# Later loads for `f2` and `fk`, and two scaled copies in another order

## The chip, the cores and the metric

One Trainium2 chip, one of its cores. The metric is device time in microseconds (us), the median of several executions. A core has five engines that run their own instruction streams and meet only at semaphores: TensorE (PE, matmuls; PEld is its weight load), VectorE (DVE), ScalarE (ACT), GpSimd (POOL) and SyncE (SP), which here only waits and issues DMAs.

## The reference

Three blocks follow each other on `x` (2 batches of 128 rows by 512), each added to its input:

```python
x = x + xattn(layernorm(x), ctx)   # self attention, cross attention over 2048 context rows, MLP
x = x + rwkv7(layernorm(x))        # T=2: the two batches are the two time steps of a recurrence
x = x + ffn(layernorm(x))          # 8 heads, 5 value experts and 5 output experts, top 2

# MLP at the end of xattn
z = relu(x @ fc1_w + fc1_b);  z = z @ fc2_w + fc2_b;  x = layer_norm(x + z)

# rwkv7, per step
r, w, k, v, a, g = (mix_m(x) @ W_m for m in "rwkvag")   # mix_m(x) = x + (xprev - x) * mu_m
...                                   # state update, y
y = y * sigmoid(g) @ Wo
h = layernorm(x + y) * norm_w + norm_b
out = layernorm(silu(h @ Wf + bf)) * lnf_w + lnf_b
```

All of it is float32. Some products are computed as three products of rounded halves (high times high, high times low, low times high); `parted` is that form, `natural` the plain float32 one.

## The kernel before

The whole program is one pass with no outer loop; the order on each engine is written out by hand, and each step waits on a semaphore count (`Flag.at(name)`) of what it needs. Batches are `0` and `1`, and steps of the two are interleaved.

**Weights and context** come in as blocks of 128 by 2048 floats (1 MB). They lie in 13 places of a ring in SBUF. `fetch(name)` on SP waits until the block that lay in that place before has been used by its last product, then issues the DMA. SP is in order: a fetch that waits holds all later ones. The places that matter: `f2` is in place 5 after context block `c01`; `rg` in 2 after `c12`; `rv` in 1 after `c11`; `ro` in 8 after `v2`; `rw` in 3, `rr` in 0; `fo` in 5 after `f2`; `rf` in 6 after `rk`; `fk` in 4 after `f1`; `fg` in 3 after `rw`; `fq` in 9, whose old content is read by step `v`. Vectors (biases, norms) are broadcast to 128 partitions in `bc`; the last such load (L401, flag `s_bc2`, 768 KB, called bc2 here) holds `lnf_b`, `norm_w` and `norm_b` and follows `fk` in SP's stream, with `fq` and `fg` after it. DVE waits for `s_bc2` in `norm_h(0)` (L1192, its work is L915), PE ahead of the bias row of `rf(0)` (L847), POOL ahead of adding `lnf_b` (L2057).

**Around the MLP**, PE runs `f1(0)`, `v2(1)`, `f2(0)`, then turns batch 1 and runs `f1(1)`, `f2(1)`. `f2(0)` (L629) waits for the block `f2` and feeds `add3(0)` on DVE (L1073).

**In the recurrence**, PE runs `step(0,"v")`, `step(1,"w")`, `step(1,"r")`, `step(1,"v")`, `step(0,"g")`, `lift(0)`, `step(1,"g")`, then turns `yg(0)`, `lift(1)`, `ro(0)`, turns `yg(1)`, `ro(1)`, turns `h(0)`, the bias row and `rf(0)` (L835 to L850). A step for `g` needs its mixed rows: for batch 0 ACT writes them alone (`mix0("g", 4)`, four scaled copies of 128 by 128, and it waits for `step(0,"v")`), for batch 1 ACT writes a first term (`mix1("g", 5)`, four copies, it waits for `step(1,"r")`) and POOL adds the second (L2038 to L2040). Behind them on ACT stand `row_high("bf", ...)` (rounds the bias row), `scales0()` (eight small copies that DVE's L1479 needs), a square, `own_part()`, `tanh(0,"g")`, `bonus_rows(1)`, `tanh(1,"g")` and the copies of the turned `yg`.

The product with `Wo` is `parted`: its first eight matmuls use the high rows, which ACT has copied; its last four wait for the low rows from DVE (`low_halves`, L1103). DVE's own order there is L1484, L1497, ..., L1521, L1103 for batch 0, L1525, L1183, L1188, then L915 and L921 (the norm of `h(0)`), L1111 (low half of the bias row).

Of the kernel before, what the change touches and what calls it, by code (L numbers as in the profile page):

```python
# [80 lines left out]
def build(nc, blocks, xin, vecs, cols, out):  # L81
    with ExitStack() as ctx:
# [31 lines left out]
        v, a, g, t = nc.vector, nc.scalar, nc.gpsimd, nc.tensor  # L114
# [25 lines left out]
        def bcols(w, b):  # L140
            return w[:, :, b * 128:(b + 1) * 128]
# [4 lines left out]
        def quarters(n):  # L146
            return psum[:, n, :].rearrange("p (c n) -> p c n", c=4)
# [7 lines left out]
        def vec(name):  # L155
            i = BCAST.index(name)
            return bc[:, i if i < FIRST_BC else i - FIRST_BC, :]
# [70 lines left out]
        def flags(name, *orders):  # L228
            return [Flag(sem(f"{name}{b}"), orders[b if len(orders) > 1 else 0]) for b in range(2)]
# [74 lines left out]
        prod = flags("product", ["k1", "q1.a", "q1", "e1", "n1", "v1", "em", "pv", "q2.a", "q2", "k2", "n2", "v2",  # L304
# [20 lines left out]
        def product(name):  # L325

            return name[1] if name in ("rk", "ra", "rw", "rr", "rv", "rg") else name

        def used(name):

            if name.startswith("ct"):
                return score[int(name[2])].at(name[3])
            if name[0] == "c":
                return gath[int(name[1])].at(name[2])
            return prod[1].at(product(name))
# [5 lines left out]
        @block_.sync  # L341
        def _(eng):
            s = Waits(eng)

            def fetch(name, first=False):
                before = [m for m in BLOCKS if PLACE[m] == PLACE[name] and NTH[m] == NTH[name] - 1]
                for m in before:
                    s.wait_ge(*used(m))
                    if m[0] != "c" and m != "rw":
                        s.wait_ge(*prod[0].at(product(m)))  # L350
                eng.dma_start(ring[:, PLACE[name], :], blocks[BLOCKS.index(name), :, :]).then_inc(
                    s_place[PLACE[name]], 16)

            def spread(first, end):
                return vecs[first:end, :].unsqueeze(0).broadcast_to([128, end - first, 512])

            eng.dma_start(X[0][:, 0:256], xin[0, :, 0:256]).then_inc(s_x[0], 16)
            fetch("k1")
            eng.dma_start(X[1], xin[1, :, :]).then_inc(s_x[1], 16)
            fetch("q1")  # L360
            fetch("ct01")
            eng.dma_start(colv[:, :], cols).then_inc(s_cols, 16)
            fetch("v1")
            fetch("ct00")
            fetch("q2")
            fetch("ct02")
            eng.dma_start(bc[:, 0:2, :], spread(0, 2)).then_inc(s_bc0, 16)
            fetch("ct10")
            fetch("k2")
            eng.dma_start(bc[:, 2:FIRST_BC, :], spread(2, FIRST_BC)).then_inc(s_bc1, 16)  # L370
            fetch("ct03")
            fetch("ct11")
            fetch("c03")
            fetch("ct12")
            fetch("c01")
            fetch("v2")
            fetch("ct13")
            fetch("c00")
            fetch("c10")
            fetch("c02")  # L380
            fetch("f1")
            fetch("c12")
            fetch("c11")
            fetch("c13")
            s.wait_ge(*normed[0].at("x1"))
            s.wait_ge(*normed[1].at("x1"))
            eng.dma_start(bc[:, 0:2, :], spread(FIRST_BC, FIRST_BC + 2)).then_inc(s_bf, 16)
            fetch("rk")
            fetch("ra")
            fetch("f2")  # L390
            fetch("rg")
            fetch("rv")
            fetch("ro")
            fetch("rw")
            fetch("rr")
            fetch("fo")
            fetch("rf")
            fetch("fk")
            s.wait_ge(*normed[0].at("n4"))
            s.wait_ge(*normed[1].at("n4"))  # L400
            eng.dma_start(bc[:, 2:len(BCAST) - FIRST_BC, :], spread(FIRST_BC + 2, len(BCAST))).then_inc(s_bc2, 16)  # L401
            for b in range(2):
                s.wait_ge(*prod[b].at("v"))
            fetch("fq")
            fetch("fg")
            s.wait_ge(*out_v[0].at("fin"))
            eng.dma_start(out[0, :, :], X[0]).then_inc(s_y[0], 16)
            s.wait_ge(*out_v[1].at("fin.a"))
            eng.dma_start(out[1, :, 0:256], X[1][:, 0:256]).then_inc(s_y[1], 16)
            s.wait_ge(*out_v[1].at("fin"))  # L410
            eng.dma_start(out[1, :, 256:512], X[1][:, 256:512]).then_inc(s_y[1], 16)
            s.wait_ge(s_y[0], 16)
            s.wait_ge(s_y[1], 32)
# [1180 lines left out]
        def _(eng):  # L1594
            s = Waits(eng)

            def act(o, x, func, **kw):
                return a.activation(o, x, func, **kw)  # L1598
# [48 lines left out]
            def row_high(name, loaded_):  # L1647

                i, p = row_parts[name]
                s.wait_ge(*loaded_)  # L1650
                act(bc_r[p:p + 64, i, :], vec(name)[p:p + 64, :], ACT.Copy).then_inc(*rows_a.inc(name))
# [32 lines left out]
            def mix0(m, n):  # L1684

                dst = HIGH_r[0][n % 2] if m in STEPS else MIX[0][n % 2].rearrange("p (c n) -> p c n", c=4)
                k = MUS.index(m)
                s.wait_ge(*(turn if n < 2 else turned)[0].at("n4"))
                s.wait_ge(*rest_v.at("rest"))
                if n > 1:  # L1690
                    s.wait_ge(*prod[0].at(["a", "k", "v", "r", "g"][n - 2]))
                src = bcols(T8, 0) if n > 1 else quarters(0)
                for c in range(4):
                    i = act(dst[:, c, :], src[:, c, :], ACT.Copy, scale=rest[:, 4 * k + c:4 * k + c + 1])
                i.then_inc(*mixed[0].inc(m))

            def mix1(m, n):
                dst = PART[1][n % 2] if m in STEPS else MIX[1][n % 2].rearrange("p (c n) -> p c n", c=4)
                k = MUS.index(m)
                s.wait_ge(*x_sum[1].at("n4"))  # L1700
                s.wait_ge(*prod[1].at("k" if m == "v" else ["k", "a", "w", "r", "v", "g"][n - 2]))
                for c in range(4):
                    i = act(dst[:, c, :], bcols(T10, 1)[:, c, :], ACT.Copy, scale=colv[:, 4 * k + c:4 * k + c + 1])
                i.then_inc(*mixed[1].inc(m))
# [10 lines left out]
            def by_head(b, name, o_, x, factor):  # L1715
                for h in range(8):
                    cs = slice(h * 64, (h + 1) * 64)
                    i = act(o_[:, cs], x[:, cs], ACT.Copy, scale=factor[:, h:h + 1])
                i.then_inc(*by_a[b].inc(name))

            def bonus_rows(b):
                s.wait_ge(*rk_v[b].at("sb"))
                s.wait_ge(*rk_v[b].at("vc"))
                by_head(b, "pv", v_p[b], v_p[b], sbs[b])

            def scales0():
                s.wait_ge(*rk_g[0].at("rs"))
                s.wait_ge(*rk_v[0].at("km"))
                by_head(0, "sc", y_p[0], vec("lnx_w"), rs8[0])
# [138 lines left out]
            act(w1, w1, ACT.Exp, bias=wbias[:, :], scale=WC).then_inc(*sq_a[1].inc("wexp"))  # L1868
            round_step("v", 4)
            bonus_rows(0)  # L1870
            mix0("g", 4)
            mix1("g", 5)
            s.wait_ge(*x2b_g[0].at("x2b"))
            s.wait_ge(*x2b_g[1].at("x2b"))
            row_high("bf", (s_bf, 16))
            scales0()
            s.wait_ge(*rk_v[1].at("km"))
            s.wait_ge(*rk_v[1].at("vc"))
# [254 lines left out]
```

## Time and profile before

| what | value |
|---|---|
| median of 3 runs (lowest, highest) | 225.9 us (225.85, 226.06) |
| the profiled execution's own time | 225.85 us |
| its span | 224.1 us |
| PE busy | 215.2 us, 96% |
| DVE busy | 175.9 us, 79% |
| ACT busy | 112.8 us, 50% |
| POOL busy | 102.1 us, 46% |
| DMA | 43.99 MB, mean 196 GB/s |
| granted PE clock | full in all 40 slices |
| chain that ended last | PE 78%, DVE 12%, POOL 3%, ACT 2%, issue 2%, DMA 1% |

The span runs from the first to the last recorded instruction; 1.75 us of the execution lie outside it. Rows below give the start in us from the span's start. A row of the timeline merges neighbours of one kind; a number in brackets is the idle time ahead of them and what ended it. Each float32 matmul shows as two records.

### The profile page before, as it was taken

What the parts mean: (1) busy time and instruction counts of PE and PEld (TensorE: products, weight loads), DVE (VectorE), ACT (ScalarE), POOL (GpSimd) and SP (SyncE); (2) the same over time, 40 slices, a digit from 0 to 9 for tenths busy, and PEclk for the clock granted to TensorE, in tenths of its full rate; (3) what the DMA queues carried; (4) which work ended last, traced back from release to release, by engine and by line L of the source; (5) the groups of instructions that cost most, each with busy time, mean ns of one, the idle gap of its engine ahead of it and who ended that gap; (6) DMA issues with size and microseconds to landing.
All of it is one profiled execution on the core that took longest, in us unless ns stands there. A gap on an engine that the chain in (4) does not pass through costs nothing.

```text
span 224.1 us, 3249 instructions
## 1 busy us (share of the span) xinstructions
PE 215.2 (96%) x1201; PEld 169.7 (76%) x1201; DVE 175.9 (79%) x320; ACT 112.8 (50%) x217; POOL 102.1 (46%) x90
## 2 busy tenths in 40 slices
PE   8899999999999999999999999999889899999995
PEld 7898889789988888888575757564466679798863
DVE  2156883877598988799689896799999899898971
ACT  2347522383689768944435287899413111246110
POOL 5016004760568336989440109979576218160000
PEclk9999999999999999999999999999999999999999
DMA  6999999159984499927390406608100000000002
GB/s 238 431 419 415 429 437 399 50 218 427 331 342 186 140 427 388 426 72 332 101 437 32 183 0 240 275 0 317 61 0 0 0 0 3 0 1 3 0 19 75
DMA packets 6783, 43.99 MB, mean 196 GB/s; under 512 B 880, under 2 KB 1392, under 8 KB 2032
## 3 DMA queue, kind: packets, MB, share of 16 engines
q1 hardware_dynamic: 6624, 43.66, 48.9%
q8 instruction: 9, 0.15, 0.3%
q10 hardware_dynamic: 144, 0.13, 0.2%
q14 instruction: 6, 0.05, 0.1%
HBM read 43.27 MB, written 0.52 MB: 195 GB/s over the span
## 4 chain that ended last, share of the span: by engine, by line
PE 78%; DVE 12%; POOL 3%; ACT 2%; issue 2%; DMA 1%; DVEq 0%; POOLq 0%
PE psum L422 57%; PE psum L464 15%; PE psum L426 4%; ACT slots L1598 2%; PE psum L438 1%; DVE small L905 1%; DMA slots<-xin 1%; POOL small L2049 1%; POOL small L2033 1%; PE psum L598 1%; POOL small L1921 1%; DVE slots L911 1%; DVE slots L927 1%; DVE slots L915 1%; DVE small L1159 1%
## 5 line engine op out<-in xcount | busy, mean ns | idle before, releaser
L422 PE MATMUL psum<-ring_r,slots_r 128*128 128x512 f32 x360 | 88.6, 399 | 1.7 <-DVE slots_r L1103 1.3
L422 PEld LDWEIGHTS psum<-ring_r,slots_r 128*128 128x128 f32 x360 | 66.2, 188 | 20.1 <-ACT slots_r L1598 2.9
L1926 POOL TENSOR_TENSOR ring_r<-ring,ring_r 128x640 fp32r<-128x640 f32 x21 | 43.4, 2079 | 27.6 <-ACT ring_r L1598 27.6
L1598 ACT ACTIVATE slots<-psum 128x256 f32<-128x256 f32 (+4 forms) x48 | 20.3, 452 | 59.1 <-PE psum L422 22.1
L1598 ACT ACTIVATE ring_r<-ring 128x2048 fp32r<-128x2048 f32 x23 | 43.8, 1915 | 10.4 <-PE psum L422 9.2
L422 PE MATMUL psum<-ring,slots 128*128 128x512 f32 (+5 forms) x122 | 41.4, 482 | 0.3 <-ACT slots L1598 0.3
L933 DVE TENSOR_TENSOR ring_r<-ring,ring_r 128x1408 fp32r<-128x1408 f32 x21 | 35.8, 1708 | 3.0 <-ACT ring_r L1598 2.9
L464 PE MATMUL psum<-slots,ring 128*128 128x128 f32 x320 | 37.6, 277 | 0.3 <-ACT slots L1598 0.3
L464 PEld LDWEIGHTS psum<-slots,ring 128*128 128x128 f32 x320 | 36.5, 192 | 0.9 <-ACT slots L1598 0.7
L422 PEld LDWEIGHTS psum<-ring,slots 128*128 128x128 f32 (+1 forms) x122 | 20.1, 190 | 14.7 <-issue 11.0
L1921 POOL TENSOR_TENSOR small<-small,mhalf 128x1 f32<-128x1 f32 x16 | 8.8, 550 | 43.0 <-DVE small L907 41.5
L1598 ACT ACTIVATE slots_r<-psum 128x512 fp32r<-128x512 f32 (+1 forms) x20 | 9.3, 509 | 14.0 <-PE psum L438 8.6
L1936 POOL TENSOR_TENSOR slots<-slots,bc 128x512 f32<-128x512 f32 x9 | 12.6, 1405 | 8.2 <-DMA bc<-vecs 6.9
L422 PEld LDWEIGHTS psum<-slots,ring 128*128 128x128 f32 x128 | 14.6, 192 | 0.4
L422 PE MATMUL psum<-slots,ring 128*128 128x128 f32 x128 | 14.9, 276 | 0.0
L1598 ACT ACTIVATE slots<-psum,small 128x128 f32<-128x128 f32 (+1 forms) x20 | 8.8, 529 | 8.6 <-DVE small L1265 5.9
L1932 POOL TENSOR_TENSOR ring_r<-ring,ring_r 128x704 fp32r<-128x704 f32 (+1 forms) x6 | 9.8, 1647 | 6.4 <-ACT ring_r L1598 6.4
L426 PE MATMUL psum<-ident,slots 128*128 128x128 f32 x68 | 9.6, 277 | 1.0 <-DVE slots L911 0.6
L1936 POOL TENSOR_TENSOR slots<-slots 128x512 f32<-128x512 f32 x8 | 10.1, 1275 | 0.3 <-DVE small L1474 0.2
L426 PEld LDWEIGHTS psum<-ident,slots 128*128 128x128 f32 x68 | 7.6, 140 | 2.5 <-DVE slots L911 1.1
L1943 POOL TENSOR_TENSOR slots<-slots,small 128x512 f32<-128x512 f32 x4 | 5.6, 1420 | 7.1 <-DVE small L1240 7.1
L438 PE MATMUL psum<-ident,slots 128*128 128x128 f32 x44 | 7.0, 281 | 1.7 <-DVE slots L911 1.2
(179 smaller groups left out, 253.8 us busy)
## 6 DMA issues: line engine op xcount, KB each, us to landing
ring<-blocks SPq DMA_DIRECT2D x36, 1024.0 KB, 7.3
bc<-vecs SPq DMA_DIRECT2D x1, 3072.0 KB, 16.1
bc<-vecs SPq DMA_DIRECT2D x2, 512.0 KB, 15.5
bc<-vecs SPq DMA_DIRECT2D x1, 768.0 KB, 8.4
slots<-xin SPq DMA_DIRECT2D x1, 256.0 KB, 5.1
y<-slots SPq DMA_DIRECT2D x1, 256.0 KB, 2.0
y<-slots SPq DMA_DIRECT2D x2, 128.0 KB, 1.7
slots<-xin ACTq DMA_DIRECT2D x1, 128.0 KB, 2.9
```

What stands on the lines that cost most here:

```text
L422: return t.matmul(o_, l, r, start=first, stop=last)
L426: i = t.transpose(o_[:, c * 128:(c + 1) * 128], x[:, c * 128:(c + 1) * 128], ident[:, :])
L438: i = t.transpose(psum[:, bk1 if c > 1 else bk0, o_ * 128:(o_ + 1) * 128], src[:, c * 128:(c + 1) * 128], ident[:, :])
L464: i = t.matmul(psum[:, bk, e * 128:(e + 1) * 128], w[:, c, e * 128:(e + 1) * 128], srcw[:, c, b * 128:(b + 1) * 128], start=c == 0 and (e ...
L598: i = t.matmul(bank(4 * b + n), pick_r[:, n, :], pen_r[b], start=False, stop=True, skip_group_check=True)
L933: v.tensor_tensor(ring_r[:, p, 0:CUT], ring[:, p, 0:CUT], ring_r[:, high(name), 0:CUT], ALU.subtract).then_inc(*split_low.inc(name))
L1598: return a.activation(o, x, func, **kw)
L1921: g.tensor_tensor(rs[b], mv[b][:, 1:2], mhalf[:, 0:1], ALU.pow).then_inc(*rstd[b].inc(name))
L1926: g.tensor_tensor(ring_r[:, p, CUT:], ring[:, p, CUT:], ring_r[:, high(name), CUT:], ALU.subtract).then_inc(*split_lowg.inc(name))
L1932: g.tensor_tensor(ring_r[:, PLACE[name], at_], ring[:, PLACE[name], at_], ring_r[:, high(name), at_], ALU.subtract).then_inc(*split_lowg.i ...
L1936: g.tensor_tensor(o, x, y, op).then_inc(*flag.inc(name))
L1943: return g.tensor_tensor(heads(dst), x_, w_, ALU.mult)
```

## The change

On SP, the fetch of `f2` goes behind those of `rg` and `rv`, and the fetch of `fk`, with everything behind it (bc2, `fq`, `fg`), waits for both products `g`. On ACT, the scaled copies `mix0("g", 4)` go behind `mix1("g", 5)` and `row_high("bf", ...)`.

```diff
@@ SP @@
             fetch("rk")
             fetch("ra")
-            fetch("f2")
             fetch("rg")
             fetch("rv")
+            fetch("f2")
             fetch("ro")
             fetch("rw")
             fetch("rr")
             fetch("fo")
             fetch("rf")
+            for b in range(2):
+                s.wait_ge(*prod[b].at("g"))
             fetch("fk")
             s.wait_ge(*normed[0].at("n4"))
             s.wait_ge(*normed[1].at("n4"))
@@ ACT @@
             bonus_rows(0)
-            mix0("g", 4)
             mix1("g", 5)
             s.wait_ge(*x2b_g[0].at("x2b"))
             s.wait_ge(*x2b_g[1].at("x2b"))
             row_high("bf", (s_bf, 16))
+            mix0("g", 4)
             scales0()
```

## Rows read from the trace of the kernel before

**Rows 1.** The chain that ended last, in order: start, us, what.
```profile
106.25 6.21 PE psum L422 x20
...
168.58 3.42 PE psum L422 x13
```

**Rows 2.** Timeline of SP: start, us, queue, line, what, count.
```profile
98.65 0.80 SPq L351 DMA_DIRECT2D ring<-blocks  x2
...
135.18 0.80 SPq L351 DMA_DIRECT2D ring<-blocks  x2
136.08 0.38 SPq L401 DMA_DIRECT2D bc<-vecs  x1
150.96 0.80 SPq L351 DMA_DIRECT2D ring<-blocks  x2
```

**Rows 3.** DMA issues by line: duration ns, first and last start, time to landing.
```profile
L351 SPq DMA_DIRECT2D ring<-blocks x5: 328/431/432, 98.7 to 109.9; - x5
...
DMA to landing us min/median/max: 4.7/6.8/8.8
...
L351 SPq DMA_DIRECT2D ring<-blocks x2: 327/376/426, 135.2 to 135.6; - x2
...
DMA to landing us min/median/max: 4.9/6.0/7.0
...
L401 SPq DMA_DIRECT2D bc<-vecs x1: 382/382/382, 136.1 to 136.1; - x1
...
DMA to landing us min/median/max: 8.4/8.4/8.4
...
L351 SPq DMA_DIRECT2D ring<-blocks x2: 327/376/426, 151.0 to 151.3; - x2
...
DMA to landing us min/median/max: 4.9/6.2/7.4
```

**Rows 4.** Timeline where `f2(0)` begins on PE (its first weight loads).
```profile
108.63 0.41 PEld L422 LDWEIGHTS psum<-ring,slots 128*128 128x128 f32 x2
```

**Rows 5.** Timeline of ACT, 148 to 156 us.
```profile
148.76 1.32 ACT L1598 ACTIVATE slots<-slots,small 128x128 f32<-128x128 f32 x4
149.93 1.31 ACT L1598 ACTIVATE slots<-slots,colv 128x128 f32<-128x128 f32 x4
151.11 0.64 ACT L1598 ACTIVATE bc_r<-bc 64x512 fp32r<-64x512 f32 x1
...
155.97 0.56 ACT L1598 ACTIVATE psum<-psum 128x512 f32<-128x512 f32 x1
```

**Rows 6.** Timeline of PE, 150 to 164 us.
```profile
150.72 3.59 PE L422 MATMUL psum<-ring,slots 128*128 128x512 f32 x8
...
154.67 3.70 PE L422 MATMUL psum<-ring,slots 128*128 128x512 f32 x8
158.21 0.60 PE L438 MATMUL psum<-ident,slots 128*128 128x128 f32 x4
...
159.33 2.11 PE L422 MATMUL psum<-ring_r,slots_r 128*128 128x512 f32 x8
162.72 1.21 PE L422 MATMUL psum<-ring_r,slots_r 128*128 128x512 f32 x4 [1.27 <-DVE slots_r L1103]
```

**Rows 7.** Timeline of DVE, 156 to 169 us.
```profile
156.23 0.68 DVE L1484 TENSOR_TENSOR slots<-slots,psum 128x512 f32<-128x512 f32 x1
...
161.99 0.68 DVE L1103 SCALAR_TENSOR_TENSOR slots_r<-psum,slots_r 128x512 fp32r<-128x512 f32 x1
...
166.12 0.74 DVE L915 SCALAR_TENSOR_TENSOR slots<-psum,small,bc 128x512 f32<-128x512 f32 x1
...
167.76 0.68 DVE L1111 TENSOR_TENSOR bc_r<-bc,bc_r 32x512 fp32r<-32x512 f32 x1
```

**Rows 8.** Busy us and instructions of each engine, clock, DMA share, GB/s.
```profile
90.00:92.00 2.00, 2.00 (x10) 1.59 (x10) 0.84 (x2) 2.00 (x2) 2.00 (x2) 1.00 1.03 434
...
96.00:98.00 2.00, 2.00 (x10) 1.66 (x9) 1.97 (x4) 0.00 (x0) 1.65 (x1) 1.00 0.00 0
```

## Prediction

> **What bounds the kernel now.** I read the chain of waits first, then the timelines of PE, ACT and DVE around the four places that the diff touches, then the DMA issues with their landings. The chain says that PE sets the end nearly everywhere, and two of its pieces matter here. From 106.25 to 112.5 us it is PE alone, through `v2(1)` and `f2(0)` [rows 1], so a late block `f2` would be paid in full. From 141 to 164 us the chain lies on DVE and POOL instead, and PE has slack there: in `ro(0)` it stands for 1.27 us until DVE's low rows (L1103) are ready [rows 6]. From 168.58 us, with the bias row and `rf(0)`, it is back on PE [rows 1], and PE and DVE then hand the work to and fro without slack. So a delay between 151 and 162 us on PE may cost nothing, while one on DVE from 162 us on is paid.
>
> **`f2` behind `rg` and `rv`.** Nothing comes earlier by it. `rg` must wait for a product of the context block before it, which ends just ahead of its issue at 98.65 us [rows 2]; `f2` had been issued before that wait and did not hold it up. Now `f2` is the third of three issues that go out together. The trace has such a trio: SP issued `ro`, `rw` and `rr` from 109.05 us on, and the third, issued at 109.9, is the slowest of the five of that stretch: it landed 8.8 us later, at 118.7 [rows 3]; that is 9.65 us after the trio's first. For `f2`: 98.65 + 9.65 = 108.30 us. PE's first weight load of `f2(0)` stands at 108.63 [rows 4]. So it is in time by 0.33 us, and I take nothing. What hides it is `v2(1)`; without that cover every tenth counts. Bounds: 0 below, since an earlier step on PE's in-order queue, `v2(1)`, holds `f2(0)` anyway. Above, the largest spacing of two landings in the rows is the pair issued at 151.0 and 151.3, landing at 155.9 and 158.7, thus 2.8 apart [rows 3]; a first landing after 4.9 and two such steps give 98.65 + 4.9 + 5.6 = 109.15, thus 0.5 us late.
>
> **`mix0("g")` behind `mix1("g")` and the bias row.** The two sets of copies and the row start on ACT at 148.76, 149.93 and 151.11 us [rows 5]; the steps from start to start are 1.17 and 1.18, shorter than the durations by 0.13 to 0.15, so I give the row of 0.64 a step of 0.52. The new order is `mix1` at 148.76, the row at 149.93, `mix0` at 150.45, done at 150.45 + 1.32 = 151.77. `mix1` doesn't wait, for its condition, `step(1,"r")`, ended before `step(1,"v")` began, and the sum of the three is unchanged, so nothing behind them on ACT moves. PE, which began `step(0,"g")` at 150.72 [rows 6], now begins at about 151.81: a gap of 1.09 us. POOL gets the rows of batch 1 about 1.2 us earlier, but step `g` of batch 1 is behind that of batch 0 on PE: no gain.
>
> Where does the 1.09 go? `step(1,"g")` moves from 154.67 to 155.76. `lift(0)`, ahead of it, is then done by about 156.0 (a product reaches SP 0.24 us after the next one starts: 150.72 on PE, 150.96 on SP [rows 2, 6]), and DVE's L1484, which needs it, starts at 156.23 [rows 7]: in time by 0.2. `tanh(0,"g")` on ACT at 155.97 [rows 5] needs the product by 155.33 + 0.24 = 155.57: in time. The turning of `yg(0)` moves from 158.21 to 159.30, and with it the tanh and copies of batch 0's rows; `ro(0)` begins at 160.42 and its eight high matmuls end at 160.42 + 2.11 = 162.53. The last four wait for DVE until 162.72 anyhow [rows 6]: L1103 begins at 161.99 and is set by DVE's and POOL's own work [rows 7]. So 1.09 us of delay goes into 1.27 us of idle time, and nothing is left, with 0.19 to spare. Bounds: 0 below (the earlier POOL add gives PE nothing), 1.09 above if the idle time is not the cover it seems.
>
> **The wait ahead of `fk`.** SP now issues `fk` when `step(1,"g")` is done. That is 159.30 + 0.24 = 159.54 us, 24.36 us later than `rf`, the first of the group of three (`rf`, `fk`, bc2), was issued [rows 2]. `rf` itself goes out at 135.18 as before. Behind the waiting fetch on SP stand bc2, `fq` and `fg`; all their other conditions hold by then. `fk`, `fq` and `fg` have time: the four transfers take, at 2.5 us a block, until about 171, and the first of the three blocks to be needed is `fg`, after `rf(0)`, which ends at 172.0 [rows 1], and two norms. The tight one is bc2. In the trace it was the third of its group: issued at 136.08, landed 8.4 later, at 144.5, thus 9.3 us after the group's first issue; in the new order it is the second. One block less in front is 135.6 + 7.0 = 142.6 minus 135.18 + 4.9 = 140.1, thus 2.5 [rows 3]. So bc2 lands 6.8 to 6.9 us after `fk` is issued: 159.54 + 6.85 = 166.4. DVE's L915 in `norm_h(0)` starts at 166.12 [rows 7] and multiplies by `norm_w`, which is in bc2. It starts 0.3 us late. The wait that was hidden by 21 us of distance now ends last there.
>
> Is the 0.3 paid? Behind L915 on DVE stand L921, whose result PE turns, and L1111 at 167.76, done at 168.44 [rows 7], which the bias row on PE at 168.58 needs [rows 1]. The slack is about 0.1 at both places, and from there on the chain has no idle time of PE that isn't DVE's own. I count 0.3 in full (0.2 would be left with the slack). Bounds: with a first landing after 4.7 instead of 4.9 (the quickest of the five in rows 3) and the slack taken, 0; with 2.8 a block, 0.7. If the 1.09 us of the ACT part were not there, `fk` would go out at 158.45, bc2 would land at 165.3, and the cost would be 0: the two edits cost something together only.
>
> The Trainium skill, DMA: Bandwidth & Descriptors, Rules for kernel authors, tells to issue a DMA early and to wait for its semaphore late, so that its fixed cost is covered; the change does the reverse for bc2, and the trace agrees that the early issue had covered it. The same page, Anatomy of one DMA, gives about 2.0 us plus bytes over 436 GB/s (fitted for DMAs from GpSimd), which for `fk` and bc2 together (1.05 and 0.79 MB) would be 6.2 us and a landing at 165.8, in time. The measured 4.9 us for a block alone, against 4.4 by that formula, speaks for my row.
>
> **Sum.** The profiled execution took 225.85 us, its span 224.1 and 1.75 around it. `f2` 0, the ACT order 0, bc2 +0.3: 226.15. The median of the runs is 0.05 above the profiled one, so as a median 226.2.
>
> **Rivals.**
>
> *bc2 in time.* The group of two is as quick as the quickest landing (4.7), or the 0.1 of slack and a product that reaches SP sooner take the rest: no change, 225.9. For it speaks that 0.3 is hardly more than the scatter of landings (4.7 to 4.9); against it that three terms would have to err the same way.
>
> *`f2` late (the other side).* Place: PE at 108.63. It decides from a landing after that time. The price is the delay itself, since the chain is on PE there: 0.5 by the bound, on top of the 0.3: 226.7. For it speaks a margin of 0.33 us under a sum of 9.65; against it that the DMA engines are idle when the trio starts, exactly as for `ro`, `rw`, `rr`.
>
> *The late `g` is not absorbed.* If PE's 1.27 us hide another need that ends only later, for instance ACT's copies of `yg(1)`, up to 1.09 is paid: 227.3 with bc2. Against it: DVE's L1103 to L1525 is gapless in time and needs nothing that moves past 160.7.
>
> *Traffic.* Behind `rf` 1.8 MB less move while DVE and POOL carry the chain. If DMA traffic slowed PE or DVE, this would give time back. PE did the same 10 matmuls in 2 us with the DMA engines at 1.03 and at 0.00 [rows 8]; so it gives nothing there. DVE and POOL have no such pair of rows; with a gain of 0.5 to 1 us in their stretch, 225.2.
>
> **Chances.** bc2 late by 0.1 to 0.6 with all else hidden: 0.47. bc2 in time: 0.17. `f2` late: 0.13. Late `g` not absorbed: 0.11. Faster through traffic or through an order that falls better: 0.12. A measurement of this kernel tells about 0.2%, or 0.45 us, from no change. Same holds bc2 in time and most (0.35) of the first case; slower the rest of it (0.12), `f2` and `g` (0.24); faster 0.12. The range 225.5 to 227.0 leaves out the better half of the last case and the worst of `g`. The likeliest case alone is 225.95 to 226.5.
>
> **What would show it.** The chain of waits with DVE's L915 of `norm_h(0)` behind a DMA of `bc`, idle for some 0.3 us; SP's `fk` at about 159.5; PE idle 1.1 us ahead of `step(0,"g")` behind ACT, and the 1.27 us of `ro(0)` shrunk to about 0.2; no idle time ahead of `f2(0)`, with the landing near 108.3. Wrong it would be if PE stood at 108.6 behind a DMA, if `ro(0)`'s last four matmuls moved past 162.8, or if the stretch from 141 to 162 us on DVE and POOL became shorter.

## The result, and the profile after

The changed kernel takes 228.73 us as a median of four runs (227.54 to 229.44), against 225.88 for the kernel before beside it (225.70 to 226.06): ratio 1.0136, 95% interval 1.0093 to 1.0179. In a later session it took 230.14 (229.67 to 230.49) against 225.94, ratio 1.0178, interval 1.0154 to 1.0202 (experiment 12). It is slower, by 3 to 4 us, where 226.2 was forecast. The runs of the first comparison lie up to 1.9 us apart, while those of before agree within 0.4 there and within 1.0 in every session. One execution of the changed kernel at 231.69 us and one of experiment 1 at 229.62 count as slow ones and stay out of the ratios.

The profiled execution took 230.31 us (span 228.6), 4.46 more than that of before. The chain of waits (start, us, what) has two pieces that weren't there, both DMAs, and a third that takes longer, a stretch of PE:

```profile
99.64 10.22 DMA ring<-blocks
109.86 0.14 issue
110.00 3.69 PE psum L424 x8
...
161.28 7.58 DMA bc<-vecs
...
168.96 0.76 DVE slots L917
...
171.44 5.02 PE psum L424 x13
```

The first is `f2`: issued at 99.64, landed 10.22 later. The second is bc2, landed at 168.86. The third is the bias row and `rf(0)`: 5.02 us for 13 matmuls, where [rows 1] has 3.42 for the same 13. Line numbers behind the edit on SP are two higher than before.

PE's timeline of the changed kernel (start, us, engine, line, what, count, idle time ahead and what ended it), against [rows 4, 6]:

```profile
110.00 3.67 PE L424 MATMUL psum<-ring,slots 128*128 128x512 f32 x8 [0.84 <-DMA ring<-blocks]
...
153.05 3.67 PE L424 MATMUL psum<-ring,slots 128*128 128x512 f32 x8 [0.98 <-issue]
...
161.74 3.31 PE L424 MATMUL psum<-ring_r,slots_r 128*128 128x512 f32 x12
165.25 0.66 PE L440 MATMUL psum<-ident,slots 128*128 128x128 f32 x4 [0.20 <-DVE slots L1185]
...
170.63 0.65 PE L440 MATMUL psum<-ident,slots 128*128 128x128 f32 x4 [1.44 <-DVE slots L923]
...
171.83 4.62 PE L424 MATMUL psum<-ring_r,slots_r 128*128 128x512 f32 x12
```

Read it by how far each piece lies behind its like of before: `v2(1)` 0.14 (106.01 before), `step(0,"g")` 2.33 (150.72), the turning of `yg(1)` 1.14 again (164.11), that of `h(0)` 2.75 (167.88). So there is a loss of about 1.0 at `f2`; a loss of 1.2 at `step(0,"g")` that is given back by 165, because `ro(0)` now runs through its 12 matmuls without the 1.27 us of idle time of [rows 6]; a loss of 1.6 ahead of `h(0)`; and one more of 1.6 inside the bias row and `rf(0)`. 0.14 + 1.0 + 1.6 + 1.6 is 4.35 of the 4.46; the last 0.1 lies between the turning of `h(0)` and the bias row.

DVE shows where the third loss begins, against the 166.12 of [rows 7]:

```profile
168.96 0.75 DVE L917 SCALAR_TENSOR_TENSOR slots<-psum,small,bc 128x512 f32<-128x512 f32 x1 [1.63 <-DMA bc<-vecs]
```

The fourth shows in the table by stretches (busy us and instructions of PE, PEld, DVE, ACT, POOL, then the granted PE clock, DMA share, GB/s):

```profile
168.00:172.00 4.00, 2.42 (x12) 1.42 (x11) 2.86 (x4) 0.66 (x2) 0.00 (x0) 1.00 0.96 407
172.00:176.00 4.00, 4.00 (x11) 3.15 (x12) 3.24 (x6) 0.00 (x0) 2.93 (x3) 0.57 0.02 8
```

PE did work for 2.42 of the 4 us and then had its clock at 0.57 of full on average, which is the lower level (1.2 GHz) for most of the stretch. By single microseconds:

```profile
172.00:173.00 1.00, 1.00 (x4) 0.82 (x5) 0.93 (x4) 0.00 (x0) 0.00 (x0) 0.71 0.06 25
...
174.00:175.00 1.00, 1.00 (x4) 0.74 (x3) 0.90 (x2) 0.00 (x0) 1.00 (x2) 0.50 0.00 0
175.00:176.00 1.00, 1.00 (x4) 0.81 (x3) 0.42 (x1) 0.00 (x0) 1.00 (x1) 0.58 0.00 0
```

The mean clock over a whole execution is on record for the executions that were not profiled too, and one stretch like this is enough to bring it to 0.993, the value of the profiled one. Of the 24 executions of the changed kernel in the record of its result, nine have 0.990 to 0.993 and took 229.32 to 231.69 us; the other fifteen have 0.997 to 1.000 and took 227.54 to 229.42. So the clock fell in some executions of this kernel and not in others, and the times of the first comparison mix the two.

### The profile page after: what moved, and what is told of

It reads as the page before. It is cut to its first block, busy times and chain, and to the rows that moved or that the text cites. A ratio compares the mean times of both kernels' runs of the same rounds, so it can differ in the third digit from the quotient of the medians.

```text
span 228.6 us, 3249 instructions
## 1 busy us (share of the span) xinstructions
PE 217.5 (95%) x1201; PEld 170.9 (75%) x1201; DVE 176.1 (77%) x320; ACT 112.9 (49%) x217; POOL 102.2 (45%) x90
## 4 chain that ended last, share of the span: by engine, by line
PE 79%; DMA 9%; DVE 6%; issue 2%; ACT 2%; POOL 1%; SPq 0%; DVEq 0%; POOLq 0%
PE psum L424 61%; PE psum L466 13%; DMA ring<-blocks 4%; DMA bc<-vecs 3%; PE psum L428 3%; ACT slots L1600 2%; DVE small L907 1%; DMA slots<-xin 1%; DVE slots L917 1%; PE psum L440 1%; PE psum L600 1%; POOL small L1923 1%; DVE slots L913 1%; DVE slots L929 1%; SPq L351 0%
## 5 line engine op out<-in xcount | busy, mean ns | idle before, releaser
L424 PE MATMUL psum<-ring_r,slots_r 128*128 128x512 f32 x360 | 90.2, 404 | 0.8 <-DVE slots_r L1105 0.4
L424 PEld LDWEIGHTS psum<-ring_r,slots_r 128*128 128x128 f32 x360 | 67.3, 191 | 19.7 <-ACT slots_r L1600 2.9
L428 PEld LDWEIGHTS psum<-ident,slots 128*128 128x128 f32 x68 | 7.6, 140 | 2.8 <-DVE slots L913 1.5
L440 PEld LDWEIGHTS psum<-ident,slots 128*128 128x128 f32 x44 | 4.9, 141 | 5.6 <-DVE slots L923 2.2
```

Of the source, the lines that this page charges most:

```text
L424: return t.matmul(o_, l, r, start=first, stop=last)
L428: i = t.transpose(o_[:, c * 128:(c + 1) * 128], x[:, c * 128:(c + 1) * 128], ident[:, :])
L440: i = t.transpose(psum[:, bk1 if c > 1 else bk0, o_ * 128:(o_ + 1) * 128], src[:, c * 128:(c + 1) * 128], ident[:, :])
```

## The experiments

Every time is a median; times of before are from the same chip and session.

**1. `f2` alone.**
```diff
-            fetch("f2")
             fetch("rg")
             fetch("rv")
+            fetch("f2")
```


> Only the fetch of f2 is moved. Theory (landings scatter and are paid): in the trace of the changed kernel f2 landed 10.2 us after its issue instead of 8.8, and PE stood 0.84 us ahead of f2(0); alone it costs the same, 1.0 us (0.6 to 1.4), 226.9, with PE idle behind a DMA there. Rival (the late landing was an accident of that execution): it lands near 108.3 us, PE does not stand, 225.9.

Measured: 226.92 against 225.99, ratio 1.0033, interval 1.0017 to 1.0049. But the times fall in two groups: 225.87, 225.99, 226.00, and six from 226.87 to 227.38. (The tenth is the 229.62; its mean clock was 0.993, against 0.998 to 1.000 in the other nine, and it has no profile.) Both theories hold, each in some executions. The profiled one was of the first group; PE's row there has no idle time:

```profile
108.96 3.59 PE L422 MATMUL psum<-ring,slots 128*128 128x512 f32 x8
```

Why two sizes? In the changed kernel, the DMA engines were nearly done at 108 us, and what still ran was about the work of one engine of 16. By stretches, first the changed kernel:

```profile
108.00:109.00 1.00, 1.00 (x6) 0.61 (x4) 0.00 (x0) 0.87 (x1) 0.06 (x1) 1.00 0.06 25
109.00:110.00 1.00, 0.16 (x1) 0.03 (x1) 0.73 (x1) 0.00 (x0) 1.00 (x1) 1.00 0.02 8
```

and then `f2` alone in its quick execution:

```profile
108.00:109.00 1.00, 1.00 (x6) 0.79 (x6) 0.00 (x0) 0.83 (x1) 0.09 (x1) 1.00 0.00 0
```

A DMA share of 0.06 is one engine of 16. The DMA queues of the changed kernel from 99.9 to 111 us (packets, MB, share of 16 engines) name what else had run meanwhile:

```profile
q1 hardware_dynamic: 441, 3.22, 75.6%
q8 instruction: 1, 0.02, 0.5%
```

Queue q8 is named `instruction`: it fetches code. The page of this execution has nine such packets with 0.15 MB together, thus about 16 KB each, and one packet runs on one engine. Its 0.5% of 16 engines over 11.1 us is 0.9 us. In the quick execution the same stretch, to 112 us, holds q1 alone, and its packet of q8 lies at 95 to 97.5 instead:

```profile
q1 hardware_dynamic: 482, 3.56, 75.4%
```
```profile
q8 instruction: 1, 0.02, 3.5%
```

The theory: a load is complete when the last of its engines is, and an engine that has fetched code in between is late by about that. Experiments 5, 6 and 8 test this. No view here tells the 16 engines apart, so that the late engine is the one that fetched isn't seen directly.

**2. The wait ahead of `fk` alone.**
```diff
             fetch("rf")
+            for b in range(2):
+                s.wait_ge(*prod[b].at("g"))
             fetch("fk")
```


> Only the wait for both products g ahead of fk is added. Without the gap on PE, fk goes out near 158.4 us. Theory (fk and bc2 take 8.0 us together, as in the trace of the changed kernel, not 6.85): bc2 lands at 166.4 and DVE's norm of h(0) starts 0.3 us late, +0.3 (0 to 0.8), 226.2. Rival (6.85 us as worked out from before): it lands at 165.3, no change. Should the PE clock fall only when bc2 is late, it stays full here.

226.52 against 225.99, ratio 1.0034 (1.0019 to 1.0049). bc2 landed 7.5 us after its issue, 7.9 after that of `fk`, and DVE stood 0.33 us for it:

```profile
167.63 0.75 DVE L917 SCALAR_TENSOR_TENSOR slots<-psum,small,bc 128x512 f32<-128x512 f32 x1 [0.33 <-DMA bc<-vecs]
```

The theory holds: there is a cost, 0.5 us where 0.3 was expected. (The profiled execution was itself 1.1 us late since 75 us, by a context block that the change doesn't touch; its row is used, its end isn't.)

**3. The order on ACT alone.**
```diff
-            mix0("g", 4)
             mix1("g", 5)
             ...
             row_high("bf", (s_bf, 16))
+            mix0("g", 4)
```


> Only mix0(g) is moved on ACT. Theory (absorbed): PE stands about 1.0 us ahead of step(0,g), the idle 1.27 us inside ro(0) shrinks to 0.1 to 0.3, and the time stays within 0.2 us of before. Rival (not absorbed): up to 1.1 us slower.

225.88 against 225.99, ratio 0.9998 (0.9988 to 1.0007): absorbed. PE stood 0.99 us ahead of the step and not at all in `ro(0)`.

**4. Wait and ACT order, `f2` as before.**

> The wait ahead of fk and the order on ACT, f2 as before. Theory (the two cost together, by the later issue of fk): fk at 159.5, bc2 at 167.5 us, DVE's norm of h(0) 1.4 us late, +1.4 (0.7 to 2.0) plus up to 1.6 where the PE clock falls in rf(0): 227.3 to 228.9. Rival (the edits are independent): the sum of the two alone, about +0.3. If the clock falls without f2's delay, the idle time ahead of h(0) is what brings it down.

227.92 against 225.99, ratio 1.0108 (1.0061 to 1.0155), 1.9 us, where the two alone give 0.5 and -0.1. They cost together, as worked out ahead. bc2 landed 7.9 us after its issue at 160.22, DVE stood 1.93 us for it, and PE 1.73 for the turning of `h(0)`:

```profile
168.18 0.75 DVE L917 SCALAR_TENSOR_TENSOR slots<-psum,small,bc 128x512 f32<-128x512 f32 x1 [1.93 <-DMA bc<-vecs]
```
```profile
169.86 0.66 PE L440 MATMUL psum<-ident,slots 128*128 128x128 f32 x4 [1.73 <-DVE slots L923]
```

The PE clock stayed full in `rf(0)` of this profiled execution all the same. One of the four times, 230.06, lies 2.1 above the middle, and it alone has a mean clock of 0.993 (the others 0.997 to 1.000).

**5. The whole change with bc2 ahead of the wait.**
```diff
             fetch("rf")
+            (waits for n4, bc2)
             for b in range(2):
                 s.wait_ge(*prod[b].at("g"))
             fetch("fk")
-            (waits for n4, bc2)
```


> The whole change, but bc2 is issued ahead of the wait for g (behind rf, as in before), only fk, fq and fg wait. Theory (only two things are paid, bc2 and f2, and the fallen PE clock follows from bc2's idle time): bc2's part goes, what stays is f2's, which comes in two sizes, 0 or 1.0 us: single times near 225.9 and 226.9 and nothing above 227.5, PE clock full in rf(0). Rival (fk, fq and fg late, or their traffic at 161 to 172 us, cost something themselves): 227.5 or more.

226.98 against 226.07, ratio 1.0026 (1.0008 to 1.0044): 225.81 to 226.10 three times, 226.90 to 227.24 seven times, none above. With bc2 back, the 1.6, the fallen clock (mean clock 0.997 to 1.000 in all ten) and the wide scatter are gone, and what is left is `f2` in its two sizes. `fk`, `fq` and `fg` late cost nothing. In the profiled execution (226.93) `f2` was late, and the queue row of 99.9 to 110 us again has the packet of code (here and in experiment 8, PE's row counts only the matmuls up to the end of the stretch that was asked for):

```profile
109.99 2.81 PE L424 MATMUL psum<-ring,slots 128*128 128x512 f32 x6 [0.81 <-DMA ring<-blocks]
```
```profile
q8 instruction: 1, 0.02, 0.6%
```

**6. Wait and ACT order as in experiment 4, PE's code shifted.** At the start PE runs matmuls on ones; as three wide ones they are 32 instructions less.
```diff
-            for _ in range(11):
-                mm(psum[:, 7, 0:128], ones[:, :], ones[:, :], True, True)
+            four = ones[:, :].unsqueeze(1).broadcast_to([128, 4, 128])
+            for _ in range(3):
+                mm(quarters(7), ones[:, :], four, True, True)
```


> Wait and ACT order as in the kernel that moved these two, but PE's 11 matmuls of 128 columns at the start are 3 of 512 columns: the same busy time with 32 instructions less, so that the code of PE is fetched later against its work. Theory (a fetch of PE's code, 16 KB on one of the 16 DMA engines, 0.9 us long, falls in the flight of fk and bc2 and makes bc2 wait for that one engine: 7.9 to 8.3 us from fk's issue, not 6.85): the fetch moves behind bc2 (past 168 us), bc2 lands 6.9 to 7.2 us after fk's issue, and the norm of h(0) is late by 0.5 instead of 1.5 to 1.9: 226.4 to 226.8. Rival (bc2 is slow by itself, or by fq and fg behind it in the queue): 8 us as before, 227.9.

226.70 against 226.07 (226.40 to 226.91), ratio 1.0023 (1.0013 to 1.0033), as the theory had it; experiment 4 had 1.0108. Between 160 us and bc2's landing, experiment 4 has the packet of code among the data, and this kernel hasn't; here it comes from 167 us on. First experiment 4, 160 to 168.2 us:

```profile
q1 hardware_dynamic: 400, 2.75, 88.0%
q8 instruction: 1, 0.02, 0.7%
```

then this kernel, 160 to 167 us, and DVE's row:

```profile
q1 hardware_dynamic: 345, 2.30, 87.7%
```
```profile
166.80 0.75 DVE L918 SCALAR_TENSOR_TENSOR slots<-psum,small,bc 128x512 f32<-128x512 f32 x1 [0.64 <-DMA bc<-vecs]
```

bc2 landed 6.6 us after its issue, 7.0 after `fk`'s: without the fetch of code, the 6.85 of the prediction is nearly what it takes. In all six profiled executions with the packet in that flight it was 7.9 to 8.3 (changed kernel and experiments 2, 4, 10, 11, 12). No instruction near bc2 was changed for it, only 32 PE instructions at the start of the program. Queue q8's packet moved with them, which is why it is taken for PE's code; and the kernel of experiment 10, with 64 instructions of PE more (3313 in all against 3249), has ten such packets in its trace instead of nine.

**7. bc2 ahead of `fk`, both behind the wait; else as experiment 4.**

> Wait and ACT order, but behind the wait bc2 is issued ahead of fk. Theory (bc2 pays for the block in front of it): it lands 4.3 to 5.3 us after its issue at 159.5, thus before 165, nothing is late, 225.9 (225.7 to 226.2). Rival (a broadcast load is slow behind any wait): lands past 166.1 and costs time.

225.90 against 226.07, ratio 0.9993 (0.9983 to 1.0003). bc2, issued at 159.82, landed 4.4 us later, at 164.2; the packet of code came after that. One exchanged line takes the whole cost away.

**8. `f2` moved, with the shifted code.**

> Only f2 moved, and PE's first matmuls as 3 of 512 columns (32 instructions less), by which the fifth fetch of PE's code came at 105.4 us. Theory (f2 is late when that fetch falls in its flight, in time when it comes at 96 us, and the two sizes of time of the kernel with f2 alone are these two cases): the fetch lies at 105 to 106, f2 lands past 109.5 and PE stands 0.7 to 1.0 us; if it lies there in every execution, no time is below 226.5. Rival (f2 scatters by itself): both sizes again, with no tie to where the fetch lies.

227.03 against 225.94, ratio 1.0045 (1.0030 to 1.0059), six times from 226.79 to 227.40 and none in the lower group. The profiled execution:

```profile
109.74 3.24 PE L422 MATMUL psum<-ring,slots 128*128 128x512 f32 x7 [0.78 <-DMA ring<-blocks]
```

So in the seven profiled executions in which `f2` goes behind `rv`, it lands late with the packet inside its flight (changed kernel, experiments 5, 8, 11 and 12) and in time without (experiments 1 and 10). That the lower group of times is always the second case isn't shown, since only one execution of each run is profiled.

**9. The kernel before with the shifted code, nothing else.**

> A control: the kernel before with PE's first matmuls as 3 of 512 columns, nothing else. Expected to equal before, 225.7 to 226.2. If it differs, the times of the two kernels with that edit are read against it.

226.12 against 225.94, ratio 1.0004 (0.9993 to 1.0015). The edit by itself moves nothing that can be told.

**10. The whole change with 16 matmuls in PE's gap.**
```diff
             ro(1)
+            for _ in range(16):
+                mm(psum[:, 2, 0:128], ones[:, :], ones[:, :], True, True)
             s.wait_ge(*normed[0].at("h"))
```


> The whole change, with 16 matmuls of 128 columns on ones put on PE between ro(1) and the turning of h(0), where PE otherwise stands for bc2 (they take about 1.8 us and leave nothing in the result). Theory (the idle time brings the PE clock down in some executions): the clock stays full in rf(0), the times above 229 go, median 228.0 to 228.4, no lower than 227.5, since bc2 is as late. Rival (the clock falls for another reason): it falls as before, median 228.7 or more.

229.78 against 226.07, ratio 1.0179 (1.0143 to 1.0215). A miss by size: the matmuls took 3.74 us, not 1.8, and held the turning of `h(0)` themselves until 171.53, 1.8 us after DVE had it ready. The mean clock was 1.000 in all four executions, but the times tell nothing of what that is worth.

**11. Seven instead of 16, and 12. the whole change once more.**

> The whole change with 7 instead of 16 matmuls on ones in the gap ahead of the turning of h(0): 7 times 0.23 us is 1.6, where the 16 took 3.7 and were themselves in the way. They leave nothing in the result. Theory (the gap lets the PE clock fall): no time above 229.2, median 228.0 to 228.6, clock full in rf(0). Rival (they don't help): times above 229.2 as in the whole change.

> The whole change once more, beside the others on one chip. By the sum of parts: 227.5 where only bc2 is late (1.5), 228.5 with f2 late (1.0), 229 to 230.3 where the PE clock falls too; median 228.5 to 229.

229.12 (228.87 to 229.40; ratio 1.0134, 1.0112 to 1.0157) with the seven, 230.14 (229.67 to 230.49; ratio 1.0178, 1.0154 to 1.0202) without, on one chip: 1.0 less, and the highest with them is below the lowest without. The mean clock was 0.998 to 1.000 in all four with the seven and 0.993 in all four without. The expectation for the seven, a median of 228.6 at most and no time above 229.2, was missed by 0.5 and 0.2. In the profiled execution with the seven (229.40) `v2(1)` already began at 106.72, 0.7 us late and ahead of all the edits; whether that holds for the other three isn't known. 172 to 176 us, first the whole change, then with the seven matmuls:

```profile
172.00:176.00 4.00, 4.00 (x12) 3.13 (x12) 3.21 (x5) 0.00 (x0) 3.01 (x3) 0.63 0.02 8
```
```profile
172.00:176.00 4.00, 3.84 (x14) 2.53 (x14) 3.80 (x6) 0.87 (x3) 2.22 (x3) 1.00 0.13 55
```

Here work in the gap kept the clock at its higher level. In the profiled execution of the repeated kernel (230.16) the parts, read from positions against before as above, are 0.1 ahead of `f2(0)`, 0.8 at `f2`, 1.8 ahead of `h(0)` and 1.7 from there to the end of `rf(0)`: 4.4 on 225.85, against 4.3 measured. Experiment 12 had been put at 228.5 to 229, with the clock as an exception; there it was the rule.

## Why the prediction was wrong, point by point

**What bounds the kernel:** right. `f2`'s lateness was paid one for one, and 1 us of PE's in the middle was not.

**`f2` in time by 0.33 us, "I take nothing":** this step failed. The forecast landing, 9.65 us after the trio's first issue, held to 0.1 us in experiment 1's quick execution (issued at 99.6, landed 8.9 later, at 108.5), and not in the changed kernel (109.86); PE stood 0.6 to 0.85 us for it in the five profiled executions in which it was late, and it cost 0.8 to 1.0 us. The one trio of the trace had no fetch of code in its flight, and the upper bound, 0.5 us, was taken from spacings instead of from what else uses the engines. The rival "`f2` late" was the right mechanism at about the right place, with a chance of 0.13 for what came in 6 of the 9 executions of experiment 1 that count, and with half the price. That experiment 1's profiled execution was in time was luck: the margin was some 0.3 us, and one packet of code takes 0.9.

**The order on ACT:** right: 1.09 us of gap foreseen, 0.97 to 1.01 seen; absorbed in `ro(0)` (experiment 3), where no idle time was left instead of the 0.2 foreseen. The rival "late `g` not absorbed" is refuted.

**The wait ahead of `fk`:** right in its mechanism, mis-sized in its term; this step failed too. `fk` at 159.54 was foreseen (159.80 in experiment 4), bc2's landing at 6.85 after it was 8.0 in the changed kernel, 7.9 and 8.3 in experiments 2 and 4, and 7.0 where the packet of code was out of the way (experiment 6). The 0.3 us was 1.6 to 1.9, and 0.6 even without the packet (experiment 6). "The two edits cost something together only" was too strong: the wait alone cost 0.5.

**The clock:** not foreseen at all; the sum has no term for it. The kernel before has a stall of 1.27 us on PE with its clock full [rows 6], and the prediction never asks what a gap does to it. Here 1.44 and 1.64 us ahead of `h(0)` (changed kernel and its repeat) were followed by the lower level through `rf(0)`, 1.6 us more, while 1.73 us in experiment 4's profiled execution were not. That the gap matters is shown by the seven matmuls (mean clock 0.998 and more in four of four, against 0.993 in four of four) and by experiments 5 to 7, where DVE stood at most 0.64 us for bc2 in the profiled executions and no mean clock lay under 0.997. What decides in which executions the clock falls stays open. Nor is a late bc2 the only way: experiment 1's 229.62 has the low mean clock too, with bc2 issued as in before; it has no profile, and its cause isn't known.

**Traffic:** nothing speaks for it. Experiment 7 has the later loads of `fk`, bc2, `fq` and `fg` and is no faster than before, to within 0.2%; the quick executions of experiment 5, with the later `fk`, `fq` and `fg`, lie at 225.81 to 226.10.

**The early issue:** The Trainium skill, DMA: Bandwidth & Descriptors, Rules for kernel authors, has it that a DMA is issued early and waited for late. The runs agree where bc2 stands behind `fk`, with 1.9 us for doing the reverse (experiment 4), and show no cost of it where bc2 goes first (experiment 7). The estimate of 6.2 us for `fk` and bc2, from the fit that the Trainium skill gives in DMA: Bandwidth & Descriptors, Anatomy of one DMA, is 0.8 under the best measured, 7.0.

## What to carry to other kernels

A landing read from one execution holds for that execution only: before moving a load towards its use, leave a margin of a microsecond or more for whatever else runs on the same DMA engines, and look at the instruction queues' packets in that stretch. When a load must be late, put the small one that is needed first ahead of the large one that isn't. The kernel before agreed within 1 us from run to run in each session; a scatter that grows after an edit, and times in separate groups above all, hint that a landing has come onto the path, or that the clock falls in some executions, which their mean granted clocks tell. No version here beats the kernel before: experiments 3 and 7 equal it.

## What the runs showed of the hardware

One fetch of code, 16 KB and 0.9 to 1.0 us on one of 16 engines in these flights, goes with loads that land later by about as much: 7.9 to 8.3 us against 7.0 for `fk` and bc2, and 9.99 to 10.24 against 8.9 and 9.1 for `f2`. The same fetch came at 95 to 97 us in some executions and at 105 to 107 in others, with the same PE program (experiments 1 and 4 against experiment 7 and the kernel before). And with 32 instructions less at the start of PE's program a later one came 4 us later (it begins between 164.5 and 165 in experiment 4 and between 168.5 and 169 in experiment 6), worth 1.2 us there. A gap of 1.44 to 1.64 us on PE was followed by the lower clock level through most of `rf(0)`, which cost 1.6; one of 1.73 us in another execution was not.
